# A staging tile of its own for the weights, GpSimd's splits moved to the end of a unit, and the gate passes dealt anew

## What is computed

```python
qkvz = (x @ W_qkvz).reshape(b_, s_, NK, 2 * DK + 2 * R * DV)
...
conv = silu(conv1d(concat(q, k, v), conv_w))          # depthwise, 4 taps
q, k = inv_scale ** 2 * rms_norm(q), inv_scale * rms_norm(k)
beta, g = sigmoid(b_gate), -exp(A_log) * softplus(a_gate + dt_bias)
...
def step(Sst, inp):
    Sst = Sst * exp(g_t)
    delta = (v_t - einsum('bhk,bhkv->bhv', k_t, Sst)) * beta_t
    Sst = Sst + k_t[..., None] * delta[:, :, None, :]
    return (Sst, einsum('bhk,bhkv->bhv', q_t, Sst))
...
return (silu(z) * rms_norm(out) * norm_w).reshape(b_, s_, VALUE_DIM) @ W_out
```

## Time and profile before

| | |
|---|---|
| median of 3 runs | 3882.16 us (3878.11 to 3885.83) |
| the profiled execution | 3868.54 us, its span 3866.8 us |
| busy: PE / PEld / DVE / ACT / POOL | 92% / 77% / 55% / 53% / 60% |
| mean granted TensorE clock | 0.972 |
| unit slots, from the first dcy (471.20 us) to the last (3507.34 us) | 3036.14 us, 63 slots |
| of it PE / PEld / DVE / ACT / POOL busy | 2920.94 / 2475.38 / 1710.75 / 1769.56 / 2177.32 us |

### The profile page before, as it was taken

One profiled execution on the slowest core, in us unless ns is written; L12 is line 12 of the kernel. 1 busy time (PEld: TensorE's weight loads), 2 busy tenths in 40 slices (PEclk: granted clock), 3 DMA queues, 4 the chain that ended last, 5 costly groups with the idle time before them and its releaser, 6 DMA issues. The chain is left out here.

```text
span 3866.8 us, 77368 instructions
## 1 busy us (share of the span) xinstructions
PE 3574.5 (92%) x29348; PEld 2990.5 (77%) x29348; DVE 2119.1 (55%) x4155; ACT 2056.0 (53%) x5168; POOL 2337.2 (60%) x2901
## 2 busy tenths in 40 slices
PE   5996599999999999999999999999999999997798
PEld 4884478888888888888888888888888888886687
DVE  4654355555555555555555555555555555553464
ACT  3432355555555555555555555555555555553343
POOL 2101477777777777777777777777777777773110
PEclk8997799999999999999999999999999999998899
DMA  4324111111111111121111121212121212111521
GB/s 159 102 36 77 56 56 68 66 68 67 67 67 67 67 67 67 67 72 65 69 66 68 63 71 62 72 62 72 62 72 62 71 63 72 61 67 40 174 56 33
DMA packets 207871, 270.43 MB, mean 70 GB/s; under 512 B 86160, under 2 KB 117264, under 8 KB 206352
## 3 DMA queue, kind: packets, MB, share of 16 engines
q1 hardware_dynamic: 202464, 250.09, 19.9%
q0 software_dynamic: 4464, 14.36, 1.0%
q10 hardware_dynamic: 576, 1.03, 0.1%
HBM read 176.12 MB, written 89.13 MB: 69 GB/s over the span
## 5 line engine op out<-in xcount | busy, mean ns | idle before, releaser
L1898 ACT ACTIVATE at_t<-at_inv 128x512 f16<-128x512 f32 x768 | 459.1, 598 | 527.8 <-PE at_inv L1707 527.6
L1486 PE MATMUL at_proj<-x_hi,at_w_hi 128*128 128x512 f32 x1024 | 441.6, 431 | 18.2 <-POOL at_w_lo L2163 18.2
L1486 PE MATMUL at_proj<-x_lo,at_w_hi 128*128 128x512 f32 x1024 | 423.5, 414 | 0.0
L1486 PE MATMUL at_proj<-x_hi,at_w_lo 128*128 128x512 f32 x1024 | 418.4, 409 | 0.0
L2088 DVE TENSOR_TENSOR at_pml<-at_prod,at_cst 128x256 f16<-128x256 f32 x768 | 322.2, 420 | 78.4 <-PE at_prod L1486 69.7
L2248 POOL TENSOR_TENSOR at_gt_lo<-at_cst,at_gates 128x512 fp32r<-128x512 f32 x256 | 261.7, 1043 | 130.3 <-PE at_misc L1486 130.3
L2059 DVE TENSOR_TENSOR at_rows<-at_misc,at_rows 128x512 f32<-128x512 f32 x256 | 177.0, 691 | 281.0 <-PE at_misc L1486 280.2
L1486 PE MATMUL at_proj<-at_w_lo,x_hi 128*128 128x256 f32 x1024 | 313.0, 306 | 0.0
L1705 PEld LDWEIGHTS at_inv<-at_pml,at_t 128*128 128x128 f16 x3072 | 206.5, 97 | 131.4 <-issue 86.4
L1486 PE MATMUL at_proj<-at_w_hi,x_hi 128*128 128x256 f32 x1024 | 306.9, 300 | 0.0
L1486 PE MATMUL at_prod<-at_t,at_nlhi 128*128 128x64 f16 (+1 forms) x3584 | 286.4, 196 | 21.3 <-ACT at_t L1896 13.2
(11 more groups left out here) (292 smaller groups left out, 10736.1 us busy)
## 6 DMA issues: line engine op xcount, KB each, us to landing
at_rows<-x SPq DMA_DIRECT2D x64, 1024.0 KB, 5.7
x<-at_rows SPq DMA_DIRECT2D x64, 1024.0 KB, 4.3
at_gb<-decays SPq DMA_DIRECT2D x64, 512.0 KB, 3.6
at_e<-w_qkvz SPq DMA_DIRECT2D x32, 512.0 KB, 3.7
ffn_weights<-ffn_w SPq DMA_DIRECT2D x1, 11776.0 KB, 36.5
ffn_w<-ffn_weights POOLq DMA_DIRECT2D x4, 2688.0 KB, 23.7
at_gb<-w_qkvz SPq DMA_DIRECT2D x16, 512.0 KB, 3.6
at_gb<-w_out SPq DMA_DIRECT2D x16, 512.0 KB, 3.5
```

The lines of the kernel that those rows point to most:

```text
L1486: return nc.tensor.matmul(out, lhsT, rhs, start=start, stop=stop)
L1898: own["a_t"].up(A(grown(t16[:, s % R].rearrange("p a t -> p (a t)"), s // R), grown(psT[s % R], s // R), ACT.Copy))
```

## The change

It adds a tile `raw` of 128 x 1024 float32. All weights of the heads after the first, and W_out, land in it, one after the other; the first head's parts land in e2, gb and raw at once. SyncE's queue is put in an order that follows: W_out once part 2 is split, part 0 once W_out is split, part 1 once part 0 is split, part 2 once part 1 is split. gb takes only decays after the first head. ScalarE no longer waits for a split before it writes e2.

On GpSimd, part 0 is split in two halves, ahead of the power of k and ahead of the second masked gate tile, in slots with j % 4 == 2. All other splits stand at the end of GpSimd's slot: part 1 in slots with j % 4 == 2, part 2 in those with j % 4 == 3, W_out in those with j % 4 == 0.

In every slot, ScalarE takes the first turned half ahead of the tap of q, which moves behind the next copy of the inverse; VectorE takes the first `low` ahead of the second tap of q. Of the 48 gate passes, step 7 now has 7 instead of 4, step 11 5 instead of 6 and step 13 5 instead of 7; steps 3 to 6, 8, 9, 10 and 12 have as many as before, though Z1 now begins in step 8 instead of 9.

```diff
@@ -1304,8 +1304,8 @@
         e2 = sb("e2", [P, R, S])
...
         gb = sb("gb", [P, R, S])
-        w_raw, w_raw2 = (t[:].rearrange("p r s -> p (r s)").rearrange("p (j n) -> p j n", j=HB) for t in (e2, gb))
-        wo_raw = gb[:]
+        raw = sb("raw", [P, R, S])
+        raw_e, raw_g, raw_w = (t[:].rearrange("p r s -> p (r s)").rearrange("p (j n) -> p j n", j=HB) for t in (e2, gb, raw))
         dcy = sb("dcy", [P, R, CH])
...
@@ -1440,41 +1440,36 @@
                     load_rows(unit + 1)
...
             load_gates(0)
-            load_part(sp, 0, 0, "l_kq", w_raw)
-            load_part(sp, 0, 1, "l_v", w_raw2)
-            sp.wait_ge(sems["p_w"], 1)
-            load_part(sp, 0, 2, "l_z", w_raw)
+            load_part(sp, 0, 0, "l_kq", raw_e)
+            load_part(sp, 0, 1, "l_v", raw_g)
+            load_part(sp, 0, 2, "l_z", raw_w)
             sp.wait_ge(sems["p_w"], 2)
...
                 first = kh * B
+                sp.wait_ge(sems["p_z"], kh + 1)
+                sp.dma_start(raw[:], w_out[kh * (R * D):(kh + 1) * (R * D), :].rearrange("(r p) n -> p r n", p=P)).then_inc(sems["l_wo"], 16)
+                load_decays(first + 1)
                 if kh + 1 < NK:
-                    sp.wait_ge(sems["p_w"], 2 * (kh + 1))
                     if kh > 0:
...
                     load_gates(kh + 1)
-                sp.wait_ge(sems["p_kg"], R * (first + 1))
-                sp.dma_start(wo_raw, w_out[kh * (R * D):(kh + 1) * (R * D), :].rearrange("(r p) n -> p r n", p=P)).then_inc(sems["l_wo"], 16)
                 next_rows(first)
-                sp.wait_ge(sems["p_wo"], R * (kh + 1))
-                load_decays(first + 1)
+                if kh + 1 < NK:
+                    sp.wait_ge(sems["p_wo"], R * (kh + 1))
+                    load_part(sp, kh + 1, 0, "l_kq", raw_w)
                 load_decays(first + 2)
                 next_rows(first + 1)
-                if kh + 1 < NK:
-                    sp.wait_ge(sems["d_aqk"], R * (first + B - 1))
-                    load_part(sp, kh + 1, 0, "l_kq", w_raw)
                 load_decays(first + 3)
...
                 if kh + 1 < NK:
-                    sp.wait_ge(sems["d_aqk"], R * (first + B))
-                    load_part(sp, kh + 1, 1, "l_v", w_raw)
-                    sp.wait_ge(sems["p_kg"], R * (first + B))
-                    load_part(sp, kh + 1, 2, "l_z", w_raw2)
+                    sp.wait_ge(sems["p_w"], 2 * kh + 3)
+                    load_part(sp, kh + 1, 1, "l_v", raw_w)
+                    sp.wait_ge(sems["p_w"], 2 * kh + 4)
+                    load_part(sp, kh + 1, 2, "l_z", raw_w)
+                    load_decays(first + B)
                 next_rows(first + 3)
-                if kh + 1 < NK:
-                    sp.wait_ge(sems["p_z"], kh + 2)
-                    load_decays(first + B)
 
...
@@ -1652,17 +1647,17 @@
                         fill[4 + 2 * h].append(lambda h=h: turn_gated(h, j - 1))
...
                     fill[6].append(gates_in(Z0_U, 15, 17))
-                    fill[7].append(gates_in(Z0_U, 17, 21))
-                    fill[8].append(gates_in(Z0_U, 21, 24))
-                    fill[9].append(gates_in(Z1_U, 0, 4))
-                    fill[10].append(gates_in(Z1_U, 4, 8))
+                    fill[7].append(gates_in(Z0_U, 17, 24))
+                    fill[8].append(gates_in(Z1_U, 0, 3))
+                    fill[9].append(gates_in(Z1_U, 3, 7))
+                    fill[10].append(gates_in(Z1_U, 7, 11))
                 if behind:
...
                 if has_delta:
-                    fill[11].append(gates_in(Z1_U, 8, 14))
-                    fill[12].append(gates_in(Z1_U, 14, 17))
-                    fill[13].append(gates_in(Z1_U, 17, 24))
+                    fill[11].append(gates_in(Z1_U, 11, 16))
+                    fill[12].append(gates_in(Z1_U, 16, 19))
+                    fill[13].append(gates_in(Z1_U, 19, 24))
                 if has_prep:
...
@@ -1877,9 +1872,7 @@
                     wait(act, "s_dg", R * j + i + 1)
...
                     if i == 0 and not has_delta:
-                        wait(act, "p_z", 1)
-                    elif i == 0 and kh + 1 < NK and j % B >= B - 2:
-                        wait(act, "p_w", 2 * (kh + 1) + j % B - B + 3)
+                        wait(act, "p_w", 1)
                     if has_delta:
...
@@ -1916,12 +1909,11 @@
                     steps[2].append(lambda: tap(K_U))
...
                     steps[2].append(lambda: tanh(V1_U, j - 1))
-                if has_prep:
-                    steps[3].append(lambda: tap(Q_U))
                 if behind:
...
                 if has_prep:
+                    steps[4].append(lambda: tap(Q_U))
                     steps[6].append(lambda: tanh(K_U))
...
@@ -2066,11 +2058,12 @@
                         steps[2 + h].append(lambda h=h: qk(h))
...
                     steps[3].append(lambda: conv(K_U, (1, 2, 3)))
+                if behind:
+                    steps[5].append(lambda: low(0, j - 1))
                 if has_prep:
-                    steps[4].append(lambda: conv(Q_U, (1,)))
+                    steps[6].append(lambda: conv(Q_U, (1,)))
                 if behind:
-                    for h in range(R):
-                        steps[5 + h].append(lambda h=h: low(h, j - 1))
+                    steps[6].append(lambda: low(1, j - 1))
                 if has_prep:
...
@@ -2153,14 +2146,15 @@
                     wait(pool, "l_taps", 48 * (kh + 1))
...
                         wait(pool, "s_proj", 4 * (kh * B - 2) + 2 + 2 * part)
-                    G.tensor_copy(cw[kh % 2][:, 2 * part:2 * part + 2, :], cw_raw[:, 2 * part:2 * part + 2, :])
+                    if hbs[0] == 0:
+                        G.tensor_copy(cw[kh % 2][:, 2 * part:2 * part + 2, :], cw_raw[:, 2 * part:2 * part + 2, :])
                 else:
...
                 at = slice(part * PART, (part + 1) * PART)
-                rows = slice(hbs[0], hbs[-1] + 1)
-                raw = w_raw2 if part == (1 if kh == 0 else 2) else w_raw
-                chain(G.tensor_copy(w_hi[:, rows, at], raw[:, rows]))
-                ins = G.tensor_tensor(w_lo[:, rows, at], raw[:, rows], w_hi[:, rows, at], ALU.subtract)
+                part_rows = slice(hbs[0], hbs[-1] + 1)
+                new = (raw_e, raw_g, raw_w)[part] if kh == 0 else raw_w
+                chain(G.tensor_copy(w_hi[:, part_rows, at], new[:, part_rows]))
+                ins = G.tensor_tensor(w_lo[:, part_rows, at], new[:, part_rows], w_hi[:, part_rows, at], ALU.subtract)
                 if hbs[-1] == HB - 1:
...
@@ -2168,8 +2162,8 @@
 
...
                 wait(pool, "s_w", WPROD * kh * B)
-                chain(G.tensor_copy(wo_hi[:, h], wo_raw[:, h]))
-                own["p_wo"].up(G.tensor_tensor(wo_lo[:, h], wo_raw[:, h], wo_hi[:, h], ALU.subtract))
+                chain(G.tensor_copy(wo_hi[:, h], raw[:, h]))
+                own["p_wo"].up(G.tensor_tensor(wo_lo[:, h], raw[:, h], wo_hi[:, h], ALU.subtract))
 
...
@@ -2219,10 +2213,6 @@
                 if has_delta:
...
                         own["p_kg"].up(G.tensor_tensor(kg[:, h, :], knT[:, P:S], gb[:, h, P:S], ALU.mult))
-                if has_prep and has_delta and (j + 1) % B == 0:
-                    split_part(kh + 1, 1)
-                if j % B == B - 2 and kh + 1 < NK:
-                    split_part(kh + 1, 0)
                 if has_delta:
...
@@ -2234,10 +2224,8 @@
                     own["p_ks"].up(last)
...
                     silu(Q_U)
-                    if j % B == 0:
-                        split_wo(kh, 0)
-                    if has_delta and j % B == B - 1:
-                        split_part(kh + 1, 2, range(HB // 2))
+                    if j % B == B - 2 and kh + 1 < NK:
+                        split_part(kh + 1, 0, range(HB // 2))
                     new_gates, at = gates_of(j + 1)
...
@@ -2262,10 +2250,8 @@
                     own["p_rk"].up(G.tensor_tensor(qs2[:, nxt, :], scale[:, nxt, CH:2 * CH], scale[:, nxt, CH:2 * CH], ALU.mult))
...
                         split_part(0, 2)
-                    if j % B == 0:
-                        split_wo(kh, 1)
-                    if has_delta and j % B == B - 1:
-                        split_part(kh + 1, 2, range(HB // 2, HB))
+                    if j % B == B - 2 and kh + 1 < NK:
+                        split_part(kh + 1, 0, range(HB // 2, HB))
                     mask_g(1)
...
@@ -2278,6 +2264,13 @@
                         chain(G.affine_select(right, nl[:, g, :].rearrange("p (c b a) -> p c b a", c=CH, a=2)[:, :, :, 1],
...
                         own["p_t0"].up(G.affine_select(right, right, [[0, CH], [-2, P // 2]], ALU.not_equal, 1.0, base=-1, channel_multiplier=1))
+                    if j % B == 0:
+                        for h in range(R):
+                            split_wo(kh, h)
+                    if j % B == B - 2 and kh + 1 < NK:
+                        split_part(kh + 1, 1)
```

(2 more changed lines are left out.)

## The result

| | before | after |
|---|---|---|
| median (range) of the timed runs | 3883.56 (3878.11 to 3885.83, 4 runs) | 3779.4 us (3778.48 to 3780.71, 4 runs) |
| the profiled execution | 3868.54, span 3866.8 | 3779.27, span 3777.5 |
| mean granted TensorE clock | 0.972 | 0.978 |
| the 63 slots from the first dcy to the last | 3036.14 | 2944.37 |

The ratio is 0.9742 (95% interval 0.9727 to 0.9758): 104 us less by the medians and 89.3 us by the two profiled executions; within the 63 slots it is 91.8 us less, and the rest of the program took 2.5 us longer. Predicted were 91 us and a median of 3791.

What follows compares the result with a forecast made beforehand. The prediction took TensorE, 92% busy, as the bound, losing time to late scaled k and short waits in each slot. 64 us (splits) plus 27 us (slots) made 91, so 3882.2 - 91 = 3791 us; range 3760 to 3825.

Steps and rivals of the forecast that it cites:

- What bounds the kernel: TensorE, 92% busy, loses 65.7 us in slots with j % 4 == 2 and 3, waiting for scaled k behind GpSimd's splits.
- Splits out of the way: Slots with j % 4 == 2 and 3: splits no longer delay the power of k; 64 us won, 0.1 left per half split.
- The rival that half of the excess has another cause: Head slots: some excess comes from elsewhere, such as DMA traffic, and half stays; 3823 us, chance 0.05.
- Splits at the end and the loads: End of GpSimd's slot: a 4.74 us hole hides the splits, leaving 1.1 and 0.8; loads land in time; cost nothing.
- the rival: End of GpSimd's slot: a split waits for its load, TensorE waits at the first turn, 4.0 each; 3975 us, chance 0.03.
- Turned half ahead of the tap: Every slot: first turned half unmoved, first low part, second turned half and first output product 0.2 us earlier; 0.21 won.
- passes dealt anew: Steps 7, 11, 13: passes fill step 7's wait; step 13 gains 0.23, step 11 nothing; with the taps 0.44 a slot, 27 us.
- The rule on the shared port: Split beside VectorE's taps of v: they might shut each other out, 1.1 us late in 46 slots; 3842 us, chance 0.05.
- The sum: Whole program: 64 us from the splits plus 27 us from the slots, 91 us; profiled execution from 3868.5 to 3777 us.
- The median: Timed runs: 91 us taken from the median of 3882.2, giving 3791 us.

Runs made afterwards that it cites:

- the change's second run: The changed kernel run once more, unaltered, in another group on another chip: 3778.6 us, ratio 0.9755 to the kernel before.
- heads only: The change with taps, low parts and gate passes put back as before, keeping the staging tile and new split places: 3803.8 us, ratio 0.9811.
- the two longer tails: The change with the subtraction of parts 1 and 2 done twice or three times at the end of GpSimd's slot: 3810.0 and 3913.0 us.
- the last experiment: The change with one gate pass moved from step 12 to step 11: 3774.4 us, ratio 0.9730, slots of 46.67.
- slots only: The kernel before with only the new taps, low parts and gate passes, weights staged as ever: 3860.5 us, ratio 0.9955.
- that with both moves: The change with one gate pass moved from step 5 to 7 and one from step 12 to 11: 3771.5 us, ratio 0.9738.
- the run with the subtraction done twice: The change with the split subtraction of parts 1 and 2 done twice at the end of GpSimd's slot, in 30 slots: 3810.0 us.

## Why the prediction was right, point by point

**What bounds the kernel: right, but one stall was missed.** The 65.7 us of excess were taken over 63 x 47.15. The first slot, at 47.08, looked plain. It has no unit behind it and so less work; it hid the same stall, as these rows of the kernel before show (its window, and TensorE's longest wait in it):

```profile
471.20:518.28 47.08, 41.39 (x392) 35.69 (x391) 22.93 (x47) 25.67 (x59) 30.39 (x38) 0.96 0.14 46
```

```profile
PE at_misc L1592 <- ACT at_kn L1867: 2.5, 1, 2.5
```

What stands ahead of the power of k there is one half of W_out's split. After the change that slot takes 43.19 us, 3.9 less, with the clock at 1.00 (42.54 in the change's second run, so the figure holds to about half a microsecond). In the kernel before TensorE was busy 41.39 us in it against 45.98 in a plain slot; comparing that column, and not the length alone, would have found it.

**Splits out of the way: right, slightly better than priced.** Slots with j % 4 = 3 fell from 51.0 us on average to 46.8, those with j % 4 = 2 from 47.72 to 46.80; the 0.1 that I left for each half split was not lost (0.27 us to spare in the timeline above). The term was 64 us; heads only show 69.0 in the slots (3036.14 to 2967.11), the difference being the first slot (3.1 there) and these tenths. The rival that half of the excess has another cause, such as DMA traffic, is out: the excess went whole when the splits moved, and with the change's loads but the old places it stayed.

**Splits at the end and the loads: right.** Costed at nothing; the holes kept 0.8 to 1.3 us, part 1 had 10.7 us from issue to use, and no wait for a load appears. That lateness would cost is shown by the two longer tails: the place that the rival names for the wait is right. Its price, 4.0 us for a stall of 2.3, was too high in the clock's part: stalls of 3.4 us on average (103.0 in 30) cost 4.4 each (130.6 in 30), so the clock added 0.9 to each and not 1.7.

**Turned half ahead of the tap, passes dealt anew: right in kind, the sizes off.** The first turned half starts 6.71 us into the slot in both kernels, as said, and the first low part and the second turned half come 0.19 earlier. The step that was mis-sized is the next one, the 0.2 passed on whole to the second low part and the first output product. These rows of the change are from the slot that starts at 890.96 (j % 4 == 1, as the slot of the earlier trace rows, which starts at 1096.19):

```profile
900.80 0.75 DVE L2044 SCALAR_TENSOR_TENSOR at_gt_lo<-at_misc,at_nw,at_gt_hi 128x512 fp32r<-128x512 f32 x1 [0.48 <-DVE at_cv_q L2001]
...
901.70 0.47 PE L1481 MATMUL at_misc<-at_wo_hi,at_gt_hi 128*128 128x512 f32 x1 [0.26 <-DVE at_gt_lo L2044]
```

The low part starts 9.84 us into the slot instead of 9.96, the output product 10.74 instead of 10.86: 0.12 earlier, and 0.13 in the other kinds of slot (10.64 instead of 10.77). The low part now has the second tap of q just ahead of it on VectorE and starts 0.06 us further behind ScalarE's half than before; why is not shown. About 0.1 is left at the product of step 12. The two passes of step 13 gave 0.21, near the 0.23 of the prediction. So a plain slot won 0.35 and not 0.44; the term of 27 us measured 22. Taps and passes on their own gave 0.13 and 0.21, which is that sum. That the pass taken from step 11 is worth nothing was right, and putting it back at the cost of step 12 is the further 0.13 of the last experiment.

**The rule on the shared port: no sign of it.** The whole splits took 2352 to 2383 ns, 2377 on average, and those of parts 1 and 2 now stand beside the three taps of v, where the earlier trace rows has 2338 to 2408:

```profile
L2157 POOL TENSOR_TENSOR at_w_lo<-at_raw,at_w_hi 128x1024 fp32r<-128x1024 f32 x31 | 73.7, 2377 | 2.6
```

The Trainium skill (SBUF — State Buffer, Who interferes with whom) names a VectorE instruction with two SBUF inputs as the one that shuts GpSimd out. The taps read PSUM, one tile and a column of weights; these rows say that they are not such.

**The sum.** 69.6 (excess and first slot) + 22 (62 slots of 0.35) = 91.6, against 91.8 seen in the slots and 91 predicted. Two errors of 5 us, a stall missed and a slot's gain overrated, cancelled each other: that the total was nearer than its terms is luck.

**The median.** The median fell by 104 and not by 91, which the sum could not give since it was made against a profiled execution 15 us faster than the runs around it. For the profiled execution it gave 3777, and 3779.3 came. How much the median falls depends on the runs of the kernel before: its four medians in this study are 3871.8, 3876.4, 3879.9 and 3883.6 us, from four groups of runs, while the change has 3778.6 and 3779.4. In the group with the lowest of them the fall is 93. The stalls may explain this too, below; what I should have asked is why this kernel's executions differ at all.

## What to carry to other kernels

Where TensorE is nearly full, look for the stall in the slots that are longer, and follow it to the first engine of its chain; then move that engine's spare work into the holes that the profile shows between its last use and the next condition, and count how much of each hole is left, because the gain hangs on that. Compare the busy column of a slot that looks plain with that of the others before taking it for plain. A filler moved within one wait changes the list of waits and not the time; moved out of a stretch that is bound into one that has to wait anyway, it is worth its length.

## What the runs showed of the hardware

The same stall of about 2.3 us has three prices. These are three slots of the kernel before with j % 4 = 3, one execution, the same work in each (columns as in the earlier trace rows):

```profile
806.24:855.94 49.70, 46.24 (x419) 39.14 (x418) 27.23 (x54) 28.16 (x75) 38.28 (x46) 1.00 0.23 75
613.10:664.19 51.09, 47.74 (x419) 40.50 (x418) 27.22 (x54) 28.17 (x75) 38.28 (x46) 0.97 0.22 73
2153.91:2206.19 52.28, 48.89 (x419) 41.71 (x418) 27.24 (x54) 28.21 (x75) 38.29 (x46) 0.93 0.21 71
```

Of the 15, three show a clock of 1.00 throughout and take 49.6 to 49.7 us, nine 0.97 and 50.9 to 51.2, three 0.93 and 52.3 to 52.4. The stall itself is worth 2.5 us over a plain slot, and the lower of the two clock levels adds 0, 1.4 or 2.6. Which of them comes is not set by the work, which is the same to the instruction, so it can differ from run to run: the timed runs of the kernel before ranged over 3869.7 to 3885.8 us in this study, at mean clocks from 0.972 for the fast ones down to 0.966, while the change stayed within 3777.4 to 3780.7. That is the likely source of the further 13 us of the median: the profiled execution of before fell at the fast end, at 0.972. It is argued from the mean clocks and not shown slot by slot. Two things speak for caution. The fastest and the slowest group of the kernel before, 3870.5 to 3877.7 and 3878.1 to 3885.8 us, do not overlap, so something that belongs to the group, such as the chip, may have a part in it. And the width of a range says little by itself: the kernel with the tile and the old places kept the stalls and stayed within 1.4 us, and that with both moves, without them, ranged over 7.8. The kernels that kept the stalls (slots only, the tile with old places) have mean clocks of 0.968 to 0.969, those without 0.975 to 0.979. The Trainium skill (TensorE: Matmul & The Clock Gate, Part 1: The HAM clock gate) has the clock drop by activity from one of two levels to the other; the rows agree on the two levels (0.50 and 1.00 in the stretches above), and they show in addition that an idle time of 2.3 us, or of 3.5, may pass without any drop. The 30 waits of up to 1.1 us in the run with the subtraction done twice all passed without one. A gap in TensorE's work should be priced with a range, not with the one slot that was looked at: I took 4.0 from a middle one, which was near the mean of 3.9 by luck.
